# Attention heads over 48 q and k rows with zeros loaded once, and small parameter loads packed into one

## What is computed

```python
# block 1 (windows of 14 x 14, 12 heads of 16 dims; 16 x 16 is padded to 28 x 28)
h = layernorm(x) ; q, k, v = windows(h) @ qkv_w + qkv_b
scores = q k^T * SCALE + rel_h(q) + rel_w(q)
x1  = x + (softmax(scores) v) @ proj_w + proj_b
out = x1 + gelu(layernorm(x1) @ fc1_w + fc1_b) @ fc2_w + fc2_b
# block 2, on out
s   = two block-diagonal layers (w1, b1, relu, w2, b2) on the transform of out
out = transform(soft_shrink(s)) / size + out
```

## Time and profile before

| | |
|---|---|
| runs | 191.21 us median of 3 (190.87 to 191.38) |
| profiled execution | 190.22 us |
| its span | 188.4 us, 4169 instructions |
| PE, DVE, ACT, POOL busy | 175.3, 112.9, 87.5, 65.7 us |
| DMA | 12958 packets, 19.45 MB; 5197 packets under 512 B |

### The profile page before, as it was taken

One profiled execution on the slowest core, in us unless ns is written; L12 is line 12 of the kernel. 1 busy time (PEld: TensorE's weight loads), 2 busy tenths in 40 slices (PEclk: granted clock), 3 DMA queues, 4 the chain that ended last, 5 costly groups with the idle time before them and its releaser, 6 DMA issues.

```text
span 188.4 us, 4169 instructions
## 1 busy us (share of the span) xinstructions
PE 175.3 (93%) x1502; PEld 153.3 (81%) x1502; DVE 112.9 (60%) x303; ACT 87.5 (46%) x230; POOL 65.7 (35%) x120
## 2 busy tenths in 40 slices
PE   7999999997998797899999999999999999999892
PEld 7766996696786675788877996878999999789892
DVE  6729675598888677587755776520111466779532
ACT  3496554934387666587785204554100223071300
POOL 1633439936055456431999521900000000000000
PEclk9999999999699999999999999999999999999999
DMA  5791227976939999957051300000012170000015
GB/s 161 210 221 25 89 79 205 225 204 180 185 105 187 218 213 205 209 115 239 12 155 41 129 0 0 0 3 0 3 43 83 42 171 0 2 0 3 0 31 138
DMA packets 12958, 19.45 MB, mean 103 GB/s; under 512 B 5197, under 2 KB 9695, under 8 KB 12938
## 3 DMA queue, kind: packets, MB, share of 16 engines
q0 software_dynamic: 3392, 10.98, 24.4%
q1 hardware_dynamic: 8810, 7.75, 17.5%
q10 hardware_dynamic: 736, 0.46, 0.9%
HBM read 6.79 MB, written 1.57 MB: 44 GB/s over the span
## 4 chain that ended last, share of the span: by engine, by line
PE 70%; DMA 9%; DVE 7%; SPq 5%; ACT 3%; issue 2%; POOL 0%; ACTq 0%; DVEq 0%; POOLq 0%
PE bank L1632 9%; PE bank L1649 8%; PE bank L1406 6%; PE bank L1474 5%; PE bank L1667 4%; DMA qop<-arena 4%; PE bank L1392 3%; SPq L607 3%; PE bank L1381 3%; PE bank L1488 3%; PE bank L1600 3%; DMA q_last<-maxt 3%; PE bank L1659 3%; PE bank L1446 3%; DMA xt<-in_x_tok 2%
## 5 line engine op out<-in xcount | busy, mean ns | idle before, releaser
L1190 DVE TENSOR_REDUCE negmax<-bank 98x2 f32<-98x392 f32 (+1 forms) x72 | 34.7, 525 | 8.8 <-PE bank L1446 8.7
L1474 PE MATMUL bank<-qop,kop 128*98 128x196 f32 (+4 forms) x140 | 22.6, 262 | 0.1
L951 ACT ACTIVATE arena<-bank 98x392 f32<-98x392 f32 x48 | 21.2, 489 | 2.5 <-PE bank L1474 2.2
L1446 PE MATMUL bank<-kop,qop 126*98 126x196 f32 x80 | 16.4, 294 | 5.3 <-DMA qop<-arena 3.8
L1474 PEld LDWEIGHTS bank<-qop,kop 128*98 128x98 f32 (+4 forms) x140 | 18.8, 176 | 0.9 <-issue 0.9
L1632 PE MATMUL bank<-h2t,wf 96*128 96x512 f32 x72 | 17.4, 398 | 0.4 <-ACT h2t L978 0.4
L1446 PEld LDWEIGHTS bank<-kop,qop 126*98 126x98 f32 x80 | 11.1, 175 | 7.3 <-issue 5.7
L1632 PEld LDWEIGHTS bank<-h2t,wf 96*128 96x128 f32 x72 | 13.3, 188 | 3.9 <-issue 0.6
L1649 PE MATMUL bank<-wf,arena 128*128 128x192 f32 x96 | 15.8, 326 | 0.0
L1649 PEld LDWEIGHTS bank<-wf,arena 128*128 128x128 f32 x96 | 15.7, 190 | 0.1
L1269 DVE TENSOR_TENSOR arena<-bank,arena 128x384 f32<-128x384 f32 x4 | 2.2, 556 | 22.1 <-PE bank L1649 22.1
(11 more groups left out here) (172 smaller groups left out, 379.5 us busy)
## 6 DMA issues: line engine op xcount, KB each, us to landing
kop<-arena POOLq DMA_DIRECT2D x20, 173.0 KB, 5.5
qop<-arena POOLq DMA_DIRECT2D x10, 227.5 KB, 6.7
qop<-arena SPq DMA_DIRECT2D x10, 130.0 KB, 2.5
qop<-arena POOLq DMA_DIRECT2D x10, 130.0 KB, 6.0
arena<-in_relw SPq DMA_DIRECT2D x2, 441.0 KB, 5.1
xt<-in_x_tok SPq DMA_DIRECT2D x4, 192.0 KB, 3.5
scratch<-arena SPq DMA_DIRECT2D x4, 192.0 KB, 2.0
k_last<-arena POOLq DMA_DIRECT2D x4, 173.0 KB, 4.8
```

The costliest lines, as they stand in the source:

```text
L951: nc.scalar.activation(pg[:, e], src[0:HWIN, 0:2 * WIN], ACT.Exp, scale=HD ** -0.5).then_inc(emptied(key), 1)
L1190: nc.vector.tensor_reduce(negmax[0:rows, n % 2, at:at + cols], ps(key)[0:rows, 0:cols * width].rearrange("p (t k) -> p t k", t=cols), AX.X ...
L1446: ins = mm(ps(key)[0:HWIN, WIN * t:WIN * t + WIN], qo(h)[0:126, c0:c0 + HWIN], ko(h)[0:126, WIN * u:WIN * u + WIN], start=True, stop=True)
L1474: ins = mm(ps(key)[0:rows, at:at + n], ko(h)[:, c0:c0 + rows], rhs, start=True, stop=True)
```

## The change

Three things are changed together.

- **48 rows.** Rows 32 to 47 now hold q low (once) against k high, and the product of q low with k low is no longer formed. Rows 48 to 63 hold zeros. TensorE still sums over 126 and 128 rows. POOL and SP load 32 + 16 rows of q and k in place of 32 + 32.
- **Zeros.** POOL sets 16 rows of `k2` (`blank`, of the second half's low part, not written until later) to zero at the start. SP, once `bv` has landed, copies them to rows 48 to 63 of all five buffers of k and of q, ahead of the row copy at L560. For the last buffer two copies follow that of k's fixed rows. PE waits for the zeros ahead of the loop over heads.
- **Parameters.** The small arrays are packed on the host into one of 128 x 308 words (`PN`), which holds what thirteen of the seventeen loads brought. POOL loads it in one transfer behind the last head's rows, then fc1's weights (the first copy) and `proj_b`, without waiting for the heads' rows to land, then after that wait the second copy of the weights, `fc2_b` and both rows of `b2`. PE, ACT and DVE wait for `params_in`; POOL waits for `pb_in` ahead of L747 and for `late_in` ahead of `bsum`.

```diff
             sp.dma_start(relw[:, 1], a["relw"][:, 1]).then_inc(relw_in[1], 16)
+            sp.wait_ge(blank_set, 1)
+            sp.wait_ge(bv_in, 16)
+            sp.dma_start(raw(kop[48:64]), raw(blank[:, None, :].to_broadcast([16, OWN, KN]))).then_inc(blank_in, 16)
+            sp.dma_start(raw(qop[48:64]), raw(blank[:, None, 0:QN].to_broadcast([16, OWN, QN]))).then_inc(blank_in, 16)
             sp.wait_ge(qrows_set, 1)
...
         def q_rows(h, part):
-            src = q2[j:j + HH * (HD - 1) + 1:HH, f, part, None, :].to_broadcast([HD, 2, QN])
-            return raw(qo(h)[32 * part:32 * part + 32]), raw(src)
+            if part == 0:
+                src = q2[j:j + HH * (HD - 1) + 1:HH, f, 0, None, :].to_broadcast([HD, 2, QN])
+                return raw(qo(h)[0:32]), raw(src)
+            return raw(qo(h)[32:48]), raw(q2[j:j + HH * (HD - 1) + 1:HH, f, 1, :])
...
-                if 2 <= h < 8:
-                    for dst, src in later_inputs[3 * (h - 2):3 * (h - 2) + 3]:
-                        sp.dma_start(dst, src, allow_slow_non_contiguous=True).then_inc(late_in, 16)
                 if h == 1:
...
                     sp.dma_start(raw(k_last[64:128, :]), raw(kop[64:128, 0])).then_inc(krows_set[OWN], 16)
+                    sp.dma_start(raw(k_last[48:64, :]), raw(kop[48:64, 0])).then_inc(krows_set[OWN], 16)
+                    sp.dma_start(raw(q_last[48:64, :]), raw(qop[48:64, 0])).then_inc(qrows_copied, 16)
                     sp.dma_start(raw(q_last[120:126, :]), raw(qop[120:126, 0])).then_inc(qrows_copied, 16)
...
+            nc.gpsimd.memset(raw(blank), 0.0).then_inc(blank_set, 1)
             pool.wait_ge(set_up, 6)
...
-                for copy in range(2):
-                    pool.dma_start(raw(ko(h)[32 * copy:32 * copy + 32]),
-                                   raw(k2[j:j + HH * (HD - 1) + 1:HH, f])).then_inc(k_loaded[h % NOK], 16)
+                pool.dma_start(raw(ko(h)[0:32]),
+                               raw(k2[j:j + HH * (HD - 1) + 1:HH, f])).then_inc(k_loaded[h % NOK], 16)
+                pool.dma_start(raw(ko(h)[32:48]),
+                               raw(k2[j:j + HH * (HD - 1) + 1:HH, f, 0])).then_inc(k_loaded[h % NOK], 16)
...
+            pool.dma_start(params[:], a["params"]).then_inc(params_in, 16)
+            for c in range(2):
+                pool.dma_start(wf1_raw[:, c], a["fc1_w"][CF * c:CF * c + CF, :]).then_inc(wf1_in, 16)
+            pool.dma_start(pb[:], a["proj_b"].partition_broadcast(128)).then_inc(pb_in, 16)
             for i in range(NOP):
                 pool.wait_ge(r_loaded[i], 16 * len(range(i, HH, NOP)))
             for h in range(NH - NOK, NH):
                 pool.wait_ge(k_loaded[h % NOK], 32 * (h // NOK + 1))
-            pool.wait_ge(late_in, 17 * 16)
-            for c in range(2):
-                pool.dma_start(wf1_raw[:, c], a["fc1_w"][CF * c:CF * c + CF, :]).then_inc(wf1_in, 16)
             for c in range(2):
                 pool.dma_start(wf1_f32[:, c], a["fc1_w"][CF * c:CF * c + CF, :]).then_inc(wf1_again, 16)
+            pool.dma_start(f2b[:], a["fc2_b"].partition_broadcast(128)).then_inc(late_in, 16)
+            pool.dma_start(b2r.rearrange("p x c -> p (x c)"),
+                           a["b2"].rearrange("x n o -> (x n o)").partition_broadcast(128)).then_inc(late_in, 16)
+            pool.wait_ge(params_in, 16)
             pool.wait_ge(wf1_in, 32)
...
+            pool.wait_ge(pb_in, 16)
             for t in range(NT):
                 nc.gpsimd.tensor_tensor(xt[:, t], xt[:, t], pb[:], ALU.add).then_inc(xpb_done, 1)
...
+            pool.wait_ge(late_in, 32)
             nc.gpsimd.tensor_tensor(bsum, b2r[:, 0], b2r[:, 1], ALU.add).then_inc(bsum_done, 1)
...
-                            pe.wait_ge(qrows_copied, 32)
+                            pe.wait_ge(qrows_copied, 48)
...
-                        pe.wait_ge(krows_set[h % NOK], 16 if h % NOK == OWN else 1)
+                        pe.wait_ge(krows_set[h % NOK], 32 if h % NOK == OWN else 1)
...
             pe.wait_ge(qrows_copied, 16)
+            pe.wait_ge(blank_in, 32)
             for n in range(NH + 3):
```

More of the change, by code:

```diff
@@ L68 @@
 CAS = C + 1
+PN = 20 + 12 * BS
 def tables():
@@ L262, in build @@
         xt = sb("xt", [128, NT, C])
-        ln2 = sb("ln2", [CF, 2, 2])
         bv = sb("bv", [128, C])
+        params = sb("params", [128, PN])
+        f1b = params[:, 0:6]
+        ln2 = params[0:CF, 6:10].rearrange("p (f s) -> p f s", f=2)
+        half4 = params[0:CF, 10:14]
+        b1c = params[0:CF, 14:18].rearrange("p (x f) -> p x f", x=2)
+        b20c = params[0:CF, 18:20]
+        w12 = params[0:CF, 20:20 + 8 * BS].rearrange("p (i x f o) -> p i x f o", i=2, x=2, f=2)
+        w2o = params[0:CF, 20 + 8 * BS:PN].rearrange("p (x f i) -> p x f i", x=2, f=2)
         pb = sb("pb", [128, C])
         f2b = sb("f2b", [128, C])
-        f1b = sb("f1b", [128, 6])
         gelu_warm = sb("gelu_warm", [128, 1])
@@ L362, in build @@
         assert QF_AT == relw_at + 2 * WS * 84 and QF_AT + QN + KN <= vaug_at - 4 * 3 * 128
+        blank = k2[0:16, 1, 1]
         def edges(h):
@@ L440, in build @@
         rows_in = sem("rows_in")
+        params_in = sem("params_in")
+        pb_in = sem("pb_in")
         late_in = sem("late_in")
@@ L449, in build @@
         qrows_copied = sem("qrows_copied")
+        blank_set = sem("blank_set")
+        blank_in = sem("blank_in")
         krows_set = [sem(f"krows_set{i}") for i in range(NOK)]
@@ L971, in _ @@
                 outputs_read(act, nc.scalar.copy, 0, bp)
-            act.wait_ge(late_in, 17 * 16)
+            act.wait_ge(params_in, 16)
             def h2_high_part(bp):
@@ L1252, in _ @@
             residual(3)
-            dve.wait_ge(late_in, 17 * 16)
+            dve.wait_ge(params_in, 16)
             dve.wait_ge(*is_full("f1c"))
-            nc.vector.tensor_tensor(f1s[:], ps("f1c")[:, 0:240:40], f1b[:], ALU.add).then_inc(emptied("f1c"), 1)
+            nc.vector.tensor_tensor(f1s[:], ps("f1c")[:, 0:240:40], f1b, ALU.add).then_inc(emptied("f1c"), 1)
             h2_low_part(0)
@@ L1569, in _ @@
                     pe.wait_ge(wbd_done, 4)
-                    pe.wait_ge(late_in, 17 * 16)
+                    pe.wait_ge(params_in, 16)
                     pe.wait_ge(*is_free("b2w"))
@@ L1771 @@
     given = {short: np.ascontiguousarray(inputs[name]) for name, short in _INS.items()}
+    fixed = tables()
     def by_dim(v):
@@ L1782, in spread, with blocks, halves @@
         return out.reshape(CF, WS, WS * HH)
-    given["w2_oi"] = np.ascontiguousarray(given["w2"].swapaxes(2, 3))
+    def blocks(w):
+        return w.reshape(2, NB // 2, BS, BS).transpose(1, 2, 0, 3).reshape(CF, 2 * BS)
+    def halves(v):
+        return v.reshape(2, CF).T
+    params = np.zeros((128, PN), np.float32)
+    params[:, 0:6] = given.pop("fc1_b").reshape(6, 128).T
+    params[0:CF, 6:10:2] = halves(given.pop("ln2_g"))
+    params[0:CF, 7:10:2] = halves(given.pop("ln2_b"))
+    params[0:CF, 10:14] = fixed.pop("half4")
+    b1, w1, w2 = given.pop("b1"), given.pop("w1"), given.pop("w2")
+    params[0:CF, 14:18] = np.concatenate([halves(b1[0]), halves(b1[1])], 1)
+    params[0:CF, 18:20] = halves(given["b2"][0])
+    turned = w2.swapaxes(2, 3)
+    params[0:CF, 20:] = np.concatenate([blocks(w) for w in (w1[0], w1[1], w2[0], w2[1], turned[0], turned[1])], 1)
+    given["params"] = params
     given["relw"] = np.stack([spread(given.pop(n)) for n in ("rel_pos_h", "rel_pos_w")], 1)
@@ L1793 @@
     given["first"][0:CF, 132:138] = given.pop("qkv_b_dj")
-    for name, v in {**given, **tables()}.items():
+    for name, v in {**given, **fixed}.items():
         arrays[f"in_{name}"] = v
```

25 lines of the change are left out of this document (removed).

## The result

| | before | after |
|---|---|---|
| median of 22 runs each | 191.24 us (188.48 to 196.04) | 189.68 us (187.67 to 192.94) |
| profiled execution | 190.22 us | 189.77 us |
| span, granted clock | 188.4 us, 0.991 | 187.7 us, 0.982 |
| DMA | 12958 packets, 19.45 MB | 9277 packets, 18.55 MB |

The ratio is 0.9934, with a 95% interval of 0.9906 to 0.9962: some 1.3 us gained, where 3.8 were forecast (the two medians differ by 1.6).

The account below looks back on a forecast made before the run. Late loads holding TensorE at 53 to 80 us were taken as the bound: -3.90 us for waits, 0 for zeros, copies and tail, plus 0.1 left over, gave -3.8 off 191.21, about 187.4 us; range 186.6 to 190.0.

Parts of the forecast that it names:

- What bounds the kernel: Scores passes, 53 to 80 us: TensorE idles beside full DMA engines; late loads cost six heads 3.90 us.
- Steps 1 and 2: Heads 5 to 11: 48-row q and k loads and small parameters off SP remove the operand waits, 3.90 us.
- the first rival: Heads' q and k loads: narrower loads save no time, only the parameters' 2.45 us go; 188.8 us, chance 0.14.
- step 1: Heads' q and k loads in 48 rows: a head falls to 682 KB, 3.34 us, below TensorE's 3.95; no wait left.
- the 0.95 I had named: Sign of being right: transfer share below 0.95 at 57 to 76 us.
- the 4.2 I hoped for: Relative rows' landing in the heads: estimated at 3.1 to 4.2 us, against 4.5 allowed.
- Step 3: Start: 757 KB of zeros take 3.7 us, in by about 21, hidden by 10 us before the first scores pass; 0.
- The slower-rate rival: Start: zeros at 40 GB/s last until 34.9 us and delay the first scores pass; 191.1 to 193.1 us, chance 0.06.
- Step 4: Last buffer's two extra SP copies, ahead of the 120:126 copy: taken as 0, with 1 us as an end.
- Step 5: Behind head 11's last load: parameters, weights and proj_b go out earlier, sharing engines only with maxima of heads 9 to 11; 0.
- the maxima become the wait: Heads at full pace: each second head waits about 1 us for maxima; gain 0.8, 190.4 us, chance 0.10.

Follow-up runs that it names:

- e7: The changed kernel with zeros written to rows 32 to 63 from 32 rows, twice the bytes, head 0's q and k loads behind them; one run, 190.51 us.
- e1: The kernel before with only q and k in 48 rows and the zeros; small parameters and weights stay where they were; ratio 0.9895.
- e2: The changed kernel with q and k back in 64 rows and no zeros, parameters packed and moved as in the change; ratio 0.9975.
- e5: The changed kernel with 16 calls (32 products) of zeros ahead of head 8's second pass; ratio 0.9981.
- e12: The changed kernel once more, unedited; ratio 0.9934.
- e8: The changed kernel with parameters, first weights and proj_b behind the wait for the last k, second weights, fc2_b and b2 behind POOL's additions; ratio 0.9759.
- e15: The same kernel as e8, measured again against the kernel before; ratio 0.9845 from five runs.
- e3: The changed kernel with parameters, fc1's first weights and proj_b issued behind POOL's wait for the last k loads; ratio 0.9885.
- e10: The changed kernel with only the second weights, fc2_b and b2 moved behind POOL's additions; ratio 0.9896.
- e9: e8 with q and k back in 64 rows and no zeros; ratio 0.9885 from four runs.
- e14: e10 with POOL's arithmetic held until the last head's maxima are split; one run, 195.89 us.
- e6: The changed kernel with q back in 64 rows, k in 48, zeros for k only; ratio 0.9924.
- e13: e8 with POOL's arithmetic held until the last head's maxima are split; ratio 0.9884.

## Why the prediction was wrong

The forecast went the right way and its range holds 189.68, but the forecast gain of 3.8 us was nearly three times the 1.3 measured.

**What bounds the kernel**: right. Late operands held six heads, and the stretch was the one to look at.

**Steps 1 and 2** (-3.9 us): right, in size too. First passes of heads 5 to 11 are at 56.55, 60.71, 64.21, 68.49, 72.41, 76.56 and 80.06, head 11's 3.70 us sooner, and six heads take 23.51 us against the 23.70 worked out. One reason was wrong, and with it a term: the half loads do not land in half the time. After's k loads and the relative rows' landings:

```profile
kop<-arena POOLq DMA_DIRECT2D x10, 173.0 KB, 3.4
...
kop<-arena POOLq DMA_DIRECT2D x10, 86.5 KB, 4.5
```

```profile
DMA to landing us min/median/max: 3.3/4.9/8.2
```

The half load also stands behind the whole one in the queue, so these two medians alone don't give its rate. The zeros do for 16 rows, 101 GB/s against 209 for 32 (e7). The Trainium skill says so in "SBUF — State Buffer", section "Door 1: The DMA port swizzle (why `[64,N]` ≈ `[32,N]`)": its table has 104 GB/s measured for partitions 0 to 15 and 189 for 0 to 31; the trace agrees with 101 and 209.

For the heads' own loads the rule of the first rival holds in part. By e1's full rate of 182 GB/s, 178 KB per us, a head of 682 KB takes 3.8 us and not the 3.34 of step 1. That is still below TensorE's 3.95, and the waits go. With the small parameters, 83 KB a head, it is 4.3, and e1 keeps its waits; by before's 205 GB/s a head of 833.5 KB takes 4.2, and e2 keeps them. These are my estimates from the windows of e1. So step 1 had the right sign with a margin of 0.1 us where it saw 0.6. The share of the transfers from 57 to 76 us is 0.82, under the 0.95 I had named. The relative rows' median is 4.9 us, neither the 4.2 I hoped for nor the 6.6 of before; it was enough because they now had 4.5 to 5.2 us before they were needed. The rival's outcome, 188.8 us by 2.45 us of gain, did not come through that rule: head 11 gained its 3.7. In operand waits neither edit suffices (3.3 us in e1, 3.5 in e2). In time e2 gained nothing and e1 as much as both together.

**Step 3** (the zeros, 0 us): mis-sized. I took 3.7 us at 209 GB/s; at 101 they take 7.7 and land 10.4 us after issue, at 26.5 and not 21. They are in before head 0 needs them, but its own loads come behind them: its first product slips by 0.1 to 2.1 us, 0.9 in the median of eleven profiled executions. How much of that reaches the end of a run isn't shown. The slower-rate rival (40 GB/s) was too dark, its mechanism there in small.

**Step 4** (the last buffer's copies, 0 us): right but for 0.2 us: head 5 waits that long for them in e5 and e7, and not in after's profile.

**Step 5 failed**: "What comes behind the last head", worth 0, since "only maxima of heads 9 to 11 share the engines". By the step's own times POOL's new loads go out at 83.31 - 5.65 - 3.9 = 73.8 us. They went out at 75.5, since head 11's relative rows, issued ahead of them, were only 2.15 us earlier than before (74.96 against 77.11) and not 3.9. I had SP's maxima at four and a half microseconds ahead of need, in the rival: head 8's at 79.54, less 3.9 at most, so 75.6 or later, behind these loads. I did not lay one beside the other. Measured, head 8's maxima are issued at 76.22, 0.7 us behind the first of them. The rival "the maxima become the wait" has the mechanism but put it in "each second head" under the heads' own traffic, where it doesn't show: in after's profile heads 5 to 7 don't wait. It is one head, 8 or 9, behind the new loads; 1.5 us in after's profile, 3.1 in e12's. And no part of the forecast priced the clock: behind the pause it is halved for some 3 us, another 1.6. Together 3.3 us of the 3.7 in the profiled execution. Taking the loads away (e1) or splitting them (e8, e15) ends wait and half clock, issuing them later (e3) leaves 0.8 us of wait, and keeping TensorE busy (e5) ends the half clock alone.

This is the account of one execution, not of the medians, which lack 2.2 to 2.5 us. The clock's part in that is smaller: after's runs behind the ratio average 0.987, and those of the kernel before beside e1 to e15 0.989 to 0.991, so before has half-clock stretches in its runs too. How the rest divides between the wait for maxima, the later start and the clock isn't shown.

A part of the same step that I had not seen at all is POOL's arithmetic coming up beside VectorE's maxima. It cost little in after's profile (a cast of 0.46 us) and up to 1.4 us in e10, where the maxima's loads were in time.

Open: what 48 rows are worth once the loads are split (nothing to 2 us, nothing in the profiled executions); whether the order of issue decides between head 8 and head 9; why a short pause halves the clock in one place and not in another; and why a dip of the clock at 48 to 54 us comes in one execution of a kernel and not in the next (0.72 in after and 1.00 in e12, the same kernel; 0.72 in before). A version with POOL's additions held but `bsum` made ahead of them wasn't tried.

## What to carry to other kernels

When transfers get off the critical path, lay every small transfer that TensorE waits for, with its lead, beside the large ones that now go out earlier: 2 KB with 4.2 us of lead were late behind 0.8 MB. Price a pause of TensorE by itself and by the clock behind it, as a cost that may or may not come: here one of 1.5 us cost 3.3, and two of the same length before cost only themselves. Halving the rows of a load need not halve its time. Where several things change together, try the parts: here packing and moving the loads (e9) brings the projection forward as far as it does together with the shorter rows (e8, e15), in the profiled executions. Loads that nobody needs for 10 us belong behind the last small one, not right behind the last large one.

## What the runs showed of the hardware

- Small transfers came in late beside large ones of another queue: 2 KB from SP's took 5.7 us in after, 6.7 in e14 and 7.8 in e12, behind POOL's 826 KB and more, where 4.45 had been enough before.
- A pause of 1.53 us was followed by a granted clock of 1.2 GHz for some 3 us (after), and so were five of 2.0 to 3.1 us (e2, e6, e7, e12, e14). Pauses of 1.56 and 1.55 (before) and 1.68 us (e9) were not. Products of zeros in the pause's place kept it at 2.4 GHz (e5).
- Zeros copied from 16 rows into 16 ran at 101 GB/s, from 32 into 32 at 209 (after, e7). With short loads of 16 rows in place of half of the q and k loads, full engines moved 182 GB/s in place of 205 (e1, before).
- VectorE's cast of 128 x 16 words took 0.17 us alone and 3.04 beside POOL's two-input operations (e10), 2.43 (e15) and 1.09 (e8), and 0.17 with POOL held (e13). The Trainium skill, "SBUF — State Buffer", section "Who interferes with whom", says that a cast can take the port pair that VectorE shares with GpSimd, and that whoever issues first has it for the whole instruction while the other blocks. The trace agrees that a cast can be held up, but the cast begun at 85.00 ended at 88.04, past the multiplication that ran until 85.25 and five of the additions (582 ns each) behind it: it was not let in at the first one's end.
- The issue of a copy on SP's queue took 3.50 us behind the zeros, 0.98 without them (after, before).
